# The candidate bias of a GRU step added by a TensorE matmul instead of by VectorE

## What is computed

```python
def cell(h, x):
    gi = x @ W_ih + b_ih
    gh = h @ W_hh + b_hh
    i_r, i_z, i_n = jnp.split(gi, 3, axis=-1)
    h_r, h_z, h_n = jnp.split(gh, 3, axis=-1)
    r = jax.nn.sigmoid(i_r + h_r)
    z = jax.nn.sigmoid(i_z + h_z)
    n = jnp.tanh(i_n + r * h_n)
    return (1.0 - z) * n + z * h
...
# experts: the top 2 of 4 by logits = hs @ Wg + bg, capacity 512 tokens each
h = gelu(tok @ W1[i]); y = h @ W2[i] * p; out = out.at[sel_idx].add(y)
```

## Time and profile before

| | us |
|---|---|
| median of 3 runs | 845.18 |
| the profiled execution, its own time | 843.71 |
| its span in the trace | 841.9 |
| TensorE busy (share of the span) | 803.9 (95%) |
| VectorE busy | 621.4 (74%) |
| ScalarE busy | 422.4 (50%) |
| GpSimd busy | 184.1 (22%) |
| mean granted TensorE clock (1 is full speed) | 0.987 |

### The profile page before, as it was taken

How to read it: one execution, slowest core, us unless ns; L and a number is a source line. 1 busy time by engine, 2 the same in 40 slices (tenths; PEclk the granted TensorE clock), 3 DMA queues, 4 the chain that set the end, 5 groups by cost and what they waited for, 6 DMA issues and landing times.

```text
span 841.9 us, 27818 instructions
## 1 busy us (share of the span) xinstructions
PE 803.9 (95%) x11573; PEld 519.2 (62%) x11574; DVE 621.4 (74%) x2104; ACT 422.4 (50%) x884; POOL 184.1 (22%) x459
## 2 busy tenths in 40 slices
PE   7999999999999999999995789999999999999996
PEld 3446656678999899999994444454445444444442
DVE  6969899869888888888888969676767576855400
ACT  0677676645566555544555437451845174417500
POOL 1002122223333333333330120221012101210011
PEclk9999999999999999999997899999999999999998
DMA  8900000000111010000001663463245324540011
GB/s 335 364 1 3 2 2 2 2 3 16 55 54 42 16 42 5 4 4 4 5 5 38 171 238 107 152 179 72 100 150 164 85 100 150 158 92 0 1 26 26
DMA packets 24281, 62.62 MB, mean 74 GB/s; under 512 B 4384, under 2 KB 4384, under 8 KB 22304
## 3 DMA queue, kind: packets, MB, share of 16 engines
q1 hardware_dynamic: 19312, 51.42, 17.7%
q0 software_dynamic: 3584, 8.42, 5.5%
q10 hardware_dynamic: 1264, 1.08, 0.4%
HBM read 52.49 MB, written 12.62 MB: 77 GB/s over the span
## 4 chain that ended last, share of the span: by engine, by line
PE 80%; DVE 12%; DMA 3%; issue 2%; ACT 2%; POOL 0%; POOLq 0%; SPq 0%; DVEq 0%; ACTq 0%
PE ps L444 23%; PE ps L660 20%; PE ps L647 18%; PE ps L436 10%; PE ps L419 3%; DVE wa L1201 3%; PE ps L454 2%; DVE wa L1206 2%; PE ps L409 2%; DVE halves L1217 2%; ACT wa L756 2%; DMA wa<-in_w 1%; DMA hx<-hs_rows,idx 1%; DVE ocand L1210 1%; PE ps L590 1%
## 5 line engine op out<-in xcount | busy, mean ns | idle before, releaser
L444 PE MATMUL ps<-halves,wa 128*128 128x64 f16 x8448 | 287.7, 193 | 5.6 <-DVE halves L1217 2.1
L444 PEld LDWEIGHTS ps<-halves,wa 128*128 128x128 f16 x8448 | 271.0, 98 | 33.1 <-DVE halves L1217 14.1
L647 PE MATMUL ps<-hx,big 128*128 128x512 f16 x768 | 167.2, 379 | 0.5 <-ACT hx L838 0.5
L660 PE MATMUL ps<-big 128*128 128x512 f16 x768 | 166.9, 379 | 0.0
L756 ACT ACTIVATE wa<-ps,un_gates 128x128 f32<-128x128 f32 x288 | 100.0, 365 | 106.7 <-PE ps L444 100.3
L647 PEld LDWEIGHTS ps<-hx,big 128*128 128x128 f16 x768 | 74.8, 98 | 90.9 <-ACT hx L838 1.5
L660 PEld LDWEIGHTS ps<-big 128*128 128x128 f16 x768 | 75.2, 98 | 89.9
L761 ACT ACTIVATE wa<-wa,un_gates 128x64 f32<-128x64 f32 x288 | 99.1, 344 | 59.9 <-DVE wa L1206 53.4
L1201 DVE SCALAR_TENSOR_TENSOR wa<-ps,bhn_s,wa 128x64 f32<-128x64 f32 x288 | 80.0, 278 | 52.9 <-ACT wa L756 52.9
L436 PE MATMUL ps<-hx,wb 128*128 128x512 f16 x432 | 106.9, 379 | 0.5 <-issue 0.5
L838 ACT ACTIVATE hx<-ps,un_hid_in 128x512 f32<-128x512 f32 x64 | 43.6, 682 | 110.2 <-PE ps L647 107.0
(11 more groups left out here) (209 smaller groups left out, 707.2 us busy)
## 6 DMA issues: line engine op xcount, KB each, us to landing
wa<-in_w SPq DMA_DIRECT2D x28, 1024.0 KB, 5.2
hs_rows<-big SPq DMA_DIRECT2D x8, 512.0 KB, 6.2
big<-in_w_hh SPq DMA_DIRECT2D x4, 768.0 KB, 19.2
wb<-in_w SPq DMA_DIRECT2D x12, 256.0 KB, 2.4
big<-in_w_ih SPq DMA_DIRECT2D x2, 1024.0 KB, 12.1
hx<-in_x_t SPq DMA_DIRECT2D x2, 1024.0 KB, 15.9
big<-in_w_ih ACTq DMA_DIRECT2D x2, 512.0 KB, 6.6
wa<-in_x_t SPq DMA_DIRECT2D x2, 512.0 KB, 6.2
```

The costliest lines, as they stand in the source:

```text
L444: mm = pe.matmul(gate_ps[:, j, g, :], whh_parts[:, k, w, (4 * g + j) * P:(4 * g + j + 1) * P], halves[:, src, k, h, :], start=False, stop= ...
L647: mm = pe.matmul(ps[:, m % 2, :], w1p[:, w, k, m * P:(m + 1) * P], tokT[:, t, k, :], start=(k == 0 and n == 0), stop=(k == KD - 1 and n == 2))
L660: mm = pe.matmul(ps[:, 2 + g % 2, :], hid[:, h, k, g * P:(g + 1) * P], w2p[:, w, k, :], start=(k == 0 and n == 0), stop=(k == KH - 1 and n ...
```

## The change

b_hn comes in as a tensor of its own, [1, 512]. Two rows of it are loaded by ScalarE's queue into partitions 0 and 32 of a buffer that VectorE has zeroed (`bhn_row`, which lies in `carried`, unused until step 20). VectorE finds the rows' peak, scales, and makes `bhn_parts` [128, 512] in fp16: the high half in row 0, in row 32 the low half, zeros elsewhere. After the low halves of the first input tiles it makes `bhn_unit` [128, 64], the scale that brings the row to the unit of the gates. In each step, right behind `inject(j)`'s matmuls, one matmul of 64 columns with `bhn_parts` as weights adds the bias to the n part; `reset` is then a plain product. `bhn_s` is gone.

```diff
+        bhn_row = carried[:, :, :, :].rearrange("p d k c -> p (d k c)")
+        bhn_parts = sb("bhn_parts", [P, D], F16)
+        bhn_unit = sb("bhn_unit", [P, COLS], BF16)
+        ROW_OF = (0, 32)
@@ inject, TensorE
                 for part in parts:
                     pe.matmul(gate_ps[:, j, 0:2, :], diag[:, :], gi_rz[:, c, j, part, :, cols],
                               start=(part == HIGH), stop=False, skip_group_check=True)
+                pe.matmul(gate_ps[:, j, 2, :], bhn_parts[:, j * P:(j + 1) * P], bhn_unit[:, :], start=False, stop=False,
+                          skip_group_check=True)
@@ TensorE, behind the 24 fill matmuls ahead of the steps
             pe.wait_ge(S["diag_ready"], 1)
+            pe.wait_ge(S["bhn_split"], 1)
@@ ScalarE, behind the small loads
             act.wait_ge(S["consts_dve"], 1)
+            for row in ROW_OF:
+                act.dma_start(bhn_row[row:row + 1, :], b_hn).then_inc(S["bhn_loaded"], 16)
@@ VectorE, first instruction
+            dve.memset(bhn_row, 0.0)
@@ VectorE, behind the peaks of the first half-chunks
                 peak_of(chunk_peak[:, k:k + 1], wih_sb[:, 2 * k:2 * k + 2, 0:D])
+            dve.wait_ge(S["bhn_loaded"], 32)
+            b_peak, b_scale, b_un = (bhn_scales[:, i:i + 1] for i in range(3))
+            link(dve.tensor_reduce(b_peak, bhn_row, AX.X, ALU.max, apply_absolute_value=True))
+            link(dve.tensor_scalar(b_peak, b_peak, 1e-30, None, ALU.max))
+            link(dve.tensor_scalar(b_un.bitcast(I32), b_peak.bitcast(I32), 0x7F800000, None, ALU.bitwise_and))
+            dve.tensor_scalar(b_scale.bitcast(I32), b_un.bitcast(I32), -1.0, float((254 + SCALE_TO) << 23),
+                              ALU.mult, ALU.add)
+            link(dve.tensor_scalar(b_un.bitcast(I32), b_un.bitcast(I32), -float(SCALE_TO << 23), None, ALU.add))
+            link(dve.tensor_scalar(bhn_parts[:, :], bhn_row, b_scale, None, ALU.mult))
+            lows_row = slice(ROW_OF[1], ROW_OF[1] + 1)
+            dve.scalar_tensor_tensor(bhn_parts[lows_row, :], bhn_row[lows_row, :], b_scale[lows_row, :],
+                                     bhn_parts[lows_row, :], ALU.mult, ALU.subtract)
             dve.wait_ge(S["wih_loaded"][1], 16)
@@ VectorE, at the scales of the gates
-            dve.tensor_scalar(bhn_s[:, :], bhh[:, 8:12], gates_scale[:, 0:1], None, ALU.mult)
@@ VectorE, behind the low halves of the first input tiles
+            dve.tensor_scalar(bhn_unit[:, :], ones[:, 0:COLS], b_un, gates_scale[:, 0:1], ALU.mult,
+                              ALU.mult).then_inc(S["bhn_split"], 1)
@@ VectorE, in each step
                     dve.wait_ge(S["sig_done"], base + j + 1)
-                    dve.scalar_tensor_tensor(rn[:, j, :], gate_ps[:, j, 2, :], bhn_s[:, j:j + 1], rz[:, j, 0, :],
-                                             ALU.add, ALU.mult).then_inc(S["rn_done"], 1)
+                    dve.tensor_tensor(rn[:, j, :], gate_ps[:, j, 2, :], rz[:, j, 0, :], ALU.mult).then_inc(S["rn_done"], 1)
```

More of the change, by code:

```diff
@@ L34, with gru_moe @@
 SEARCH_PASSES = 10
-def gru_moe(nc, x, x_t, cond_t, w_ih, w_hh, b_ih, b_hh, wg, bg, w1, w2, hs_rows, out):
+def gru_moe(nc, x, x_t, cond_t, w_ih, w_hh, b_ih, b_hh, b_hn, wg, bg, w1, w2, hs_rows, out):
     NB, T, D = x.shape
@@ L178, in gru_moe @@
         gates_scale = sb("gates_scale", [P, 1])
-        bhn_s = sb("bhn_s", [P, KD])
+        bhn_row = carried[:, :, :, :].rearrange("p d k c -> p (d k c)")
+        bhn_parts = sb("bhn_parts", [P, D], F16)
+        bhn_unit = sb("bhn_unit", [P, COLS], BF16)
+        bhn_scales = sb("bhn_scales", [P, 3])
+        ROW_OF = (0, 32)
         neg_scale = sb("neg_scale", [P, 1])
@@ L226, in gru_moe @@
             candin_ready tanh_done ocand_done start_saved check_a worst_ready worst_mm flag_ready
-            gru_over turned wg_split lg_mm lg_kept sq_done probs_in probs_stored group_made rows_copied rows_stored steps_made exp_in exp_done
+            gru_over turned bhn_loaded bhn_split wg_split lg_mm lg_kept sq_done probs_in probs_stored group_made rows_copied rows_stored steps_made exp_in exp_done
             above_ready chunk_peaks total_mm masks_ready sums_ready eq_mm sel_ready pos_mm pos_ready slots_ready list_mm idx_ready
@@ L1674, in laid_out @@
         'b_hh': np.asarray(inputs['L0_cond_b_hh']).reshape(-1, P).T,
+        'b_hn': np.asarray(inputs['L0_cond_b_hh'])[2 * d:].reshape(1, -1),
         'wg': np.asarray(inputs['L0_ffn_Wg']).reshape(kd, P, -1).transpose(1, 0, 2),
```

## The result

| | before | with the change |
|---|---|---|
| median of the runs | 845.1 us (844.33 to 845.66) | 848.29 us (847.2 to 849.18) |
| profiled execution, its span | 843.7, 841.9 us | 848.13, 846.4 us |
| mean granted clock | 0.987 | 0.98 |
| ratio with its 95% interval | | 1.0041 [1.0029, 1.0052] |

A forecast was written before the change was run, and what follows sets the result against it. The chain of waits, 80% TensorE and 12% VectorE, was taken to bound the kernel. The terms 5.1 + 2.0 + 2.8 - 5.3 - 0.1 = +4.5 us on the median 845.2 gave 849.7 us, range 845.0 to 854.5.

The forecast's parts named there:

- Part 1: Exact steps 24 to 71: reset falls from 278 to about 225 ns, 0.11 us less per step, 5.3 us less.
- the second, smaller wait: TensorE's wait in exact steps for the blend of block 1, ahead of the long run; 0.10 us.
- the tanh limit: In exact steps tanh 0 ends at 227.40 whatever the resets do, so the blend of block 0 moves by 0.09 us.
- Part 2: Four added 64-column matmuls per step: 2.8 us more in steps 0 to 23, hidden in TensorE's waits in the other 48.
- Part 3: Before the steps, VectorE waits 3.4 us for the two rows to land, at 16.1 us; bounds 0 and 5.
- the same 10.6 for the nearest load: The rows' landing time on ScalarE's queue, taken from the last small load there: 10.6 us, second row at 16.1.
- Part 4: VectorE's seven instructions before the steps take 2.6 us; with the landing wait, less later waits, TensorE starts 5.1 us later.
- Part 5: TensorE's clock falls during its idle time before the steps, costing 2.0 us; bounds 0 and 2.6.
- the first three cases: Slower outcomes: the forecast, 849.7 us (0.50); no fall of the clock, 847.7 (0.17); the loop gives nothing back, 855.0 (0.14).

The follow-up runs named there:

- e3: Kernel before with reset as a plain product and b_hn left out of the computation: 838.96 us, ratio 0.9931.
- e9: Kernel before with the plain product in reset of block 3 only, b_hn left out there: 844.42 us, ratio 1.0.
- e11: Kernel before with an unread memset of 32 elements ahead of GpSimd's low halves: 843.78 us, ratio 0.9986.
- e12: Kernel before with an unread memset of 384 elements on VectorE ahead of the low half of block 2: 858.53 us, ratio 1.0159.
- e2: Kernel before with a 64-column matmul of all-zero weights added behind each inject: 848.22 us, ratio 1.0039.
- e5: Changed kernel with 13 matmuls of 512 columns on ones, result overwritten, put into TensorE's wait: 846.09 us, ratio 1.0014 to the kernel before.
- e1: Changed kernel without the bias matmul and with the reset and bhn_s of before, so the preparation alone: 851.25 us, ratio 1.0075 to the kernel before.
- e6: Changed kernel with the two row loads issued ahead of ScalarE's small loads: 843.76 us, ratio 0.9989 to the kernel before.
- e4: Changed kernel with VectorE's preparation block and its wait moved behind the low halves of the first input tiles: 842.23 us, ratio 0.997 to the kernel before.
- e8: Kernel before with the plain product in resets of blocks 0 to 2 only, b_hn left out there: 838.47 us, ratio 0.9924.
- e10: Kernel before with an unread memset of 128 elements on VectorE ahead of the low half of block 2: 845.78 us, ratio 1.0014.
- e7: Changed kernel with the preparation block moved late and the bias matmul only from step 24 on: 840.9 us, ratio 0.9959 to the kernel before.

## Why the prediction was right, and where it was not

*Part 1, reset and the loop.* The size was right: 219 ns where I had 225, a cycle 0.10 us shorter where I had 0.11, and 5.37 us in all where I had 5.3. That the totals meet is in part luck: 0.10 us in each of 47 cycles is 4.7, 0.32 instead of 0.10 came once, between the sigmoids of steps 24 and 25 (5.31 before, 4.99 after and in e3), and the rest lies in a few uneven cycles. The step that failed is the way there: "Reset 3, which stands before the blend of block 1, gives up to 0.05 more for that" and "the second, smaller wait". Reset 3 gives nothing (e9), and that wait could be taken away without the cycle following (e11). What the loop waits for is VectorE's last low half, at the end of its row (e12). I had followed the chain of waits from the blends to the 63 matmuls and not asked which of those 63 needs what was made last. That the blend of block 0 can move by no more than 0.09, because of tanh 0, was about right: 0.08. It is a fit with the row's 0.10 that only resets ahead of that blend count, but no run took the tanh limit away, so the part that it plays is argued and not shown. The timeline of after, tanh 0 and `one_less_z(0)`, fits it:

```profile
229.75 0.34 ACT L770 ACTIVATE wa<-wa,un_gates 128x64 f32<-128x64 f32 x1
...
230.12 0.23 DVE L1233 SCALAR_TENSOR_TENSOR ocand<-wa 128x64 f32<-128x64 f32 x1
```

`one_less_z(0)` begins 0.03 us behind the end of tanh 0, where it began 0.12 behind in before.

*Part 2, the matmuls.* Right: 5.63 against 5.51 us per rough step, as forecast, and nothing in the exact steps (e2). The stretch up to step 24 grew by 2.2 us in after and 2.5 in e2 instead of 2.8. It holds exact steps too, in which the shorter reset counts: in e3 it is 0.8 us shorter than in before. The Trainium skill (TensorE: Matmul & The Clock Gate, Back-to-back issue gap) gives about 81 ns for pairs with 128-column matmuls; these pairs with 64 columns cost 30 ns.

*Part 3, the landing of the rows.* Right in kind, too large in size: the wait was 1.9 us and not 3.4. The step that failed is "I take the same 10.6 for the nearest load". The second row was issued near 5.5 and had landed by 14.5, about 9 us; in e5 it was 0.5 us later. The load taken as a model, issued ahead of it, was the slower one: it took 11.0 us in after. It is spread over 128 partitions, the rows are one partition each; whether that is the reason, no run shows. The other four small loads on that queue took 8.7 to 9.1 us in before, and with 9.0 us the sum gives a wait of 1.8. The 0.6 and 2 us of the Trainium skill (DMA: Bandwidth & Descriptors, Latency and other measured facts) are still far from this.

*Part 4, the seven instructions.* 2.6 us, as summed. With the shorter wait TensorE's products started 3.1 us later instead of 5.1: 1.9 + 2.6, less 1.3 that VectorE's later waits took up (I had 0.9) and the 0.1 of `bhn_s`.

*Part 5, the clock.* Right that it falls and that this is a term of its own: 2.7 us where I took 2.0, just over the bound of 2.6. In e1 a fall of the same kind cost 1.4, so the 2.7 is the price in one execution. e5 and e6 take it away in two ways, by work and by time. Idle times of 3.2 and 3.3 us went with a fall (e1, after), of 1.2 to 1.5 us without one (e4, e6, e5, e8).

*The sum.* 3.1 + 2.7 + 2.2 - 5.4 = +2.7 up to the last step, where the prediction had +4.5. The start of the products (2.0 us too much, 1.5 of it the landing) and the matmuls (0.6 too much) were partly offset by the clock (0.7 too little), so that the time came out nearer than its terms did. The medians say +3.2. The chances of the first three cases add to 0.81, not the 0.80 that the prediction has.

*What stays open.* In the profiled execution of after the routing took 2 us longer. Its timeline shows the eight matmuls on ones there, which only keep TensorE busy, at a lower clock:

```profile
497.06 2.87 PE L588 MATMUL ps<-onesb 128*128 128x512 bf16 x8
```

They took 1.89 us in before, e1, e2, e3, e8, e9, e10 and e12, and 2.9 to 3.5 in after, e4 to e7 and e11, one trace each. The whole stretch goes with it: 49.0 to 49.6 us in the first group, 51.0 to 51.6 in the second. It is not the change alone that does it, since e11 is the kernel before with a memset on GpSimd. Executions of one kernel also differ in their mean clock (0.983 to 0.988 in before, 0.980 to 0.986 in after). What decides whether the clock falls there, no run tested.

## What to carry to other kernels

Preparation that looks small costs most of its time when it stands in the row of a saturated engine ahead of the first matmul (3.1 of 4.5 us in after), and can cost nearly twice that when the idle time that it makes lets TensorE's clock fall; the same instructions behind that row cost nothing that could be told (e4). A matmul is free only where TensorE waits, so a bias moved to it should be moved only in those steps (e7). And in a loop whose engines are nearly balanced, look for the instruction made last in each row and for who needs it. The chain names the longest way round, but a pause of known length at a row's end tells whether it binds, if it is longer than what the row can take up (e12 did, e10 did not). An instruction that stands between another and the one that needs its result can be shortened without gain (e9).

## What the runs showed of the hardware that I had not expected

- A VectorE instruction is stretched by GpSimd's start: the blend of block 1 takes 0.41 us in before and 0.28 in after, and in e11, where a memset of 0.12 us moved the start of GpSimd's subtraction by 0.06 us (from 0.02 to 0.08 behind that of the blend), the blend took 0.27 and the next instruction 0.33 instead of 0.21. It reads two tensors in SBUF, as the next one does. The Trainium skill says that the two engines share their SBUF interfaces, with contention for VectorE instructions "with two SBUF inputs" (GPSIMD Engine Reference, Specifications); the trace agrees, with 0.12 to 0.13 us once per overlap. Other overlaps of the same kinds of instruction show no stretch, so when it strikes is not settled.
- A VectorE instruction that needs the result of the last but one began 0.10 to 0.11 us behind the end of that one (the blend of block 1 in five kernels, the low half of block 3 in before), and what stood between cost nothing up to that time. This is why a pause of 0.17 us in front of the two low halves was taken up almost whole (e10), and why the two take 0.41 us in before and 0.28 behind the memset.
- A product of two tensors of 64 columns takes 219 ns, the sum and product with a per-partition scalar 278: that scalar's price here is 0.06 us an instruction. `one_less_z`, which is the same operation as reset with a constant in that place, takes 0.21 us in the earlier trace rows, and the blend, which has a per-partition scalar again, 0.28.
